# A perceiver layer on one core: three value tiles in every pair's turn, the keys between the probability transposes and the scores, and rows of scales in front of the scores

## The chip, the cores and the metric

The kernel runs on one core of one Trainium2 chip. The metric is the device time of one execution in microseconds (us), as the median of several runs of the same program.

## The reference, cut to what matters

The layer adds a cross attention, a causal self attention and a feed-forward part to a state of 2 batches x 128 rows x 512. The change touches the cross attention alone:

```python
xn = layer_norm(ctx, g1, b1)               # ctx: 2 x 2048 x 512
ln_lat = layer_norm(layernorm(x), g2, b2)  # 2 x 128 x 512
q = ln_lat @ Wq                            # 16 heads of 64
k, v = split(concat([xn, ln_lat]) @ Wkv)   # 2176 keys and values per batch
w = softmax(where(mask, (q * scale) @ (k * scale).T, -max))
x = x + (w @ v) @ Wout
```

## The kernel before, in words

**Precision.** Every projection is made with operands that are split into a high and a low part (`HI`, `LO`), by three products (`product`, L1629: high x high, high x low, low x high). So whatever TensorE projects into PSUM has to be split again before it is used: ScalarE copies the high part out of PSUM (a `*_hi` function), then VectorE subtracts it from PSUM to get the low part (a `*_lo` function). Only after the second of these is the PSUM bank free.

**Stages.** The 2176 columns of a batch are cut into three splits of 5 or 6 tiles of 128 columns, so there are 6 rounds (2 batches x 3 splits, `RNDS`). A round goes over 8 pairs of heads. `ITERS` = 48 turns follow each other, turn I being pair I % 8 of round I // 8; the text below calls rounds 0 and 3 the first splits, 1 and 4 the middle ones, 2 and 5 the last ones. Softmax is made online over the splits: a running maximum, a running sum, and an output that is scaled when the maximum moves. The first split of a batch needs no scaling, the middle one scales the output (alpha), the last one also divides by the sum (1/l).

**A turn on TensorE** (L1827 to L1862) works on three pairs at once. For pair I it transposes the probabilities (`turn_probs`, four calls into the four banks of pS and pT) and, after the scores, multiplies them with the values (`outputs`). For pair I + 1 it makes the scores (`scores`, into the same four banks). For pair I + 2 it makes the keys (`project_keys`, two chunks q = 0, 1 of up to 384 columns), and for the group of two pairs G = I // 2 + 1 a share of the values (`project_value`, one tile of 128 columns of context at a time, 12 matmuls each). In round 0 it also makes the queries of pair I + 2. `rows_of_scales` (L1774) turns alpha and 1/l into rows in bank pX; ScalarE copies them out (`scale_rows`), VectorE uses them in `merge`.

**Jobs.** Keys, values and queries all go through one PSUM tensor pJ with two banks. A list of jobs (L330) fixes their order and so the bank of each: job j uses bank j % 2 and TensorE waits in `job_bank` (L1674) until VectorE has taken the low part of job j - 2 (`c_jl`). Before, a group has three value jobs V.0, V.1, V.2 of two tiles each (the last of one tile where the split has five): V.0 in the even turn, V.1 and V.2 in the odd one.

**Keys are kept once.** KT holds one pair's keys for each q. So `key_hi` (L787) waits until `scores` of the pair before, same q, is done (`c_s`), and `scores` waits for `key_lo`.

**Order on the other engines.** ScalarE, turn I (L902): four `prob_hi`, `scale_rows`, `joined_hi`, `x_hi`, `value_hi`, `exps` of pair I + 1 (two, one per head, each needing the negated maxima of VectorE), `rescale` (alpha of pair I + 1), `value_hi` of V.2, `x_hi`, two `key_hi`. VectorE (L1314): `prob_lo`, `sums` (running sum and 1/l), three `prob_lo`, four `masked_max` of pair I + 1, `negate`, `value_lo`, `merge`, `value_lo` of V.2, `key_lo`, `join`, `stats` of a context chunk in every fourth turn, `key_lo`. GpSimd (L653) normalises a chunk (`normal`), takes low parts of the context (`x_lo`) and of the outputs (`joined_lo`). `steps_of` (L373) places the transposes of the next context chunk: in turns I = 0, 1, 4, 5, 8, 9 and so on up to 37, two `x_turn` each.

**Waits that count below.** `rows_of_scales` waits for alpha, and in the last splits for 1/l (`c_rec`, the end of `sums`). `outputs` waits for `merge` of the pair before. `join` waits for `joined_lo` of the pair before (`c_ol`). `x_turn` of a chunk waits for its `normal` (`c_norm`).

```python
def job_bank(name):
    j = job[name]
    if j >= 2:
        pe.wait_ge(c_jl, j - 1)
    return pJ[:, j % 2, :]
```

Of the kernel before, what the change touches and what calls it, by code (L numbers as in the profile page):

```python
# [35 lines left out]
def perceiver_layer(nc, x, ctx1024, mask, g1, b1, g2, b2, Wq, Wkv, Wout, qw, kw, vw, ow,  # L36
# [19 lines left out]
    PAIRS = H // 2  # L56
    SPLITS = 3
# [19 lines left out]
    with ExitStack() as stack:  # L77
# [251 lines left out]

        jobs = ["Q0", "K0.0", "V0.0", "K0.1", "V0.1", "V0.2", "Q1", "K1.0", "K1.1"]  # L330
        for I in range(ITERS):
            if I // 2 + 1 < GROUPS:
                jobs += [f"V{I // 2 + 1}.{I % 2}"]
            if I % 2 and I // 2 + 1 < GROUPS:
                jobs += [f"V{I // 2 + 1}.2"]
            if I + 2 < ITERS:
                jobs += [f"K{I + 2}.0", f"K{I + 2}.1"]
            if I + 2 < PAIRS:
                jobs += [f"Q{I + 2}"]
# [6 lines left out]
        def after_values(G):  # L346
            return job[f"V{G}.2"] + 1

        def after_round(R):
            return max(after_keys(PAIRS * R + PAIRS - 1), after_values(PAIRS // 2 * R + PAIRS // 2 - 1))  # L350

        def value_tiles(G, j):
            n = 5 if G // 4 % SPLITS == SPLITS - 1 else 6
            return list(range(2 * j, min(2 * j + 2, n)))

# [25 lines left out]
        def turned_before(I):  # L381

            return 4 + 2 * sum(steps_of(i) is not None for i in range(I))

        def scaled_before(C, k):

            if C < 2:
                return 0
            return sum(i // PAIRS % SPLITS > 0 for i in range(4 * C - (8 if k < 2 else 7) + 1))

# [343 lines left out]
        def _(act):  # L734
# [157 lines left out]
            value_hi(0, 1)  # L892
            value_hi(0, 2)
            exps(0, 0)
            exps(0, 1)
# [6 lines left out]
            for I in range(ITERS):  # L902
                n, step, G = I + 1, steps_of(I), I // 2 + 1
                for h in range(2):
                    for q in range(2):
                        prob_hi(I, h, q)
                scale_rows(I)
                if I >= 2 and pair_iter(I - 2):
                    joined_hi(I - 2)
                if step:  # L910
                    x_hi(step[0], step[1])
                if G < GROUPS:
                    value_hi(G, I % 2)
                if I + 3 < PAIRS:
                    wk_hi(I + 3)
                if n < ITERS:
                    exps(n, 0)
                    exps(n, 1)
                    rescale(n)
                if I % 2 and G < GROUPS:  # L920
                    value_hi(G, 2)
                if step:
                    x_hi(step[0], step[1] + 1)
                if I + 2 < ITERS:
                    key_hi(I + 2, 0)
                    key_hi(I + 2, 1)
                if I + 2 < PAIRS:
# [180 lines left out]
        def _(dve):  # L1108
# [199 lines left out]
            value_lo(0, 1)  # L1308
            value_lo(0, 2)
            query_lo(1)  # L1310
            key_lo(1, 0)
            key_lo(1, 1)

            for I in range(ITERS):  # L1314
                n, G = I + 1, I // 2 + 1
                C9 = (I + 10) // 4 if (I + 10) % 4 == 0 else 0
                prob_lo(I, 0, 0)
                sums(I)
                prob_lo(I, 0, 1)
                prob_lo(I, 1, 0)  # L1320
                prob_lo(I, 1, 1)
                if n < ITERS:
                    for q in range(2):
                        for h in range(2):
                            masked_max(n, q, h)
                    negate(n)
                if G < GROUPS:
                    value_lo(G, I % 2)
                if (I + 2) % PAIRS == 0 and (I + 2) // PAIRS < RNDS:
                    mask_bias((I + 2) // PAIRS)  # L1330
                merge(I)
                if I % 2 and G < GROUPS:
                    value_lo(G, 2)
                if I + 2 < ITERS:
                    key_lo(I + 2, 0)
                if I >= 1 and pair_iter(I - 1):
                    join(I - 1)
                if 3 <= C9 < CHUNKS:
                    stats(C9)
                if I + 2 < ITERS:  # L1340
                    key_lo(I + 2, 1)
                if I + 2 < PAIRS:
                    query_lo(I + 2)
# [282 lines left out]
        def _(pe):  # L1626
# [177 lines left out]
            scores(0, 1)  # L1804
            for i in (1, 2):
                for t in value_tiles(0, i):
                    project_value(0, i, t)
# [19 lines left out]
            for I in range(ITERS):  # L1827
                n, step, G = I + 1, steps_of(I), I // 2 + 1
                for h in range(2):
                    for q in range(2):  # L1830
                        turn_probs(I, h, q)
                rows_of_scales(I)
                if G < GROUPS:
                    ts = value_tiles(G, I % 2)
                    project_value(G, I % 2, ts[0])
                if step:
                    x_turn(step[0], step[1])
                if G < GROUPS:
                    project_value(G, I % 2, ts[1])
                if n < ITERS:  # L1840
# [7 lines left out]
                if step:  # L1848
                    x_turn(step[0], step[1] + 1)
                if I % 2 and G < GROUPS:  # L1850
                    for t in value_tiles(G, 2):
                        project_value(G, 2, t)
                if I + 2 < ITERS:
                    project_keys(I + 2, 0)
                    project_keys(I + 2, 1)
                elif I + 2 == ITERS:
                    pe.wait_ge(c_jl, NJ)
# [259 lines left out]
```

## Time and profile before

| | |
|---|---|
| runs of the program | 977.21 us median of 3 (975.59 to 979.12) |
| the profiled execution, its own time | 979.92 us |
| its span, first to last instruction | 978.1 us |
| TensorE matmuls busy | 874.0 us, 89% of the span |
| TensorE weight loads busy | 805.8 us, 82% |
| VectorE busy | 600.2 us, 61% |
| ScalarE busy | 491.4 us, 50% |
| GpSimd busy | 313.5 us, 32% |
| DMA | 99.11 MB, mean 101 GB/s |

The loop of 48 turns runs from 57.3 to 683 us of the span. The profiled execution took 2.7 us more than the median. In a row of a timeline the first number is the start in us of the span, the second the time in us; "[2.60 <-DVE xneg L1226]" is idle time of the engine before that row and who ended it. L numbers are lines of the kernel before. Most matmuls of the loop start 0.12 us (256 columns) or 0.17 us (384 columns) after each other and their records overlap, since each record also covers the way through the array.

### The profile page before, as it was taken

The page shows a single profiled execution, that of the slowest core. Times are in us where ns is not written, and L with a number is a line of the kernel's source. Part 1 is how long each engine was busy: PE and PEld are TensorE (multiplying, and loading weights), DVE is VectorE, ACT ScalarE, POOL GpSimd, SP SyncE. Part 2 cuts the span into 40 slices and gives each one's busy share as a digit, 9 for nine tenths or more (in the row PEclk, how much of TensorE's full clock was granted, in tenths as well). Part 3 has the DMA queues.
Part 4 walks back from the last instruction along what each step waited for, and adds up shares of the span by engine and source line. Part 5 has one row for each costly group of instructions (what it writes and reads, how often), then busy time and mean ns, then how long its engine had stood idle before and what let it go on. Part 6 is the DMA issues. An engine that isn't in the chain of part 4 may idle for free.

```text
span 978.1 us, 16973 instructions
## 1 busy us (share of the span) xinstructions
PE 874.0 (89%) x6217; PEld 805.8 (82%) x6217; DVE 600.2 (61%) x1550; ACT 491.4 (50%) x1051; POOL 313.5 (32%) x284
## 2 busy tenths in 40 slices
PE   3799999999998899999999999888687787978997
PEld 2699999999987888999999998887464586867885
DVE  6345546666657666555656666556286377865785
ACT  3465554645454554545454644454557154444553
POOL 3534522120202213131212000220726358753443
PEclk9799999999999999999999999999695888989999
DMA  5165321322323232322122223314220513421320
GB/s 191 58 222 184 123 98 65 109 90 87 108 90 128 72 122 91 120 91 99 69 82 90 87 87 133 123 40 145 100 87 0 188 47 126 130 86 64 109 87 22
DMA packets 45219, 99.11 MB, mean 101 GB/s; under 512 B 3745, under 2 KB 16977, under 8 KB 41937
## 3 DMA queue, kind: packets, MB, share of 16 engines
q1 hardware_dynamic: 45040, 98.00, 28.8%
q8 instruction: 50, 0.82, 0.3%
q14 instruction: 33, 0.26, 0.1%
q10 hardware_dynamic: 96, 0.02, 0.0%
HBM read 88.06 MB, written 8.91 MB: 99 GB/s over the span
## 4 chain that ended last, share of the span: by engine, by line
PE 75%; DVE 11%; issue 5%; ACT 4%; POOL 3%; DMA 1%; SPq 0%; DVEq 0%; ACTq 0%
PE pJ L1631 14%; PE pJ L1632 14%; PE pJ L1633 14%; PE pV L1770 7%; PE pS L1748 3%; PE pT L1756 3%; PE pS L1756 3%; PE pT L1748 2%; POOL WS L586 2%; PE pS L1631 2%; DVE KV L1119 2%; PE pS L1633 2%; PE pS L1632 2%; PE pX L1671 1%; PE pX L1787 1%
## 5 line engine op out<-in xcount | busy, mean ns | idle before, releaser
L1631 PE MATMUL pJ<-WV,XT 128*128 128x256 f32 x544 | 161.6, 297 | 0.0
L1632 PE MATMUL pJ<-WV,XT 128*128 128x256 f32 x544 | 154.9, 285 | 0.0
L1633 PE MATMUL pJ<-WV,XT 128*128 128x256 f32 x544 | 154.7, 284 | 0.0
L815 ACT ACTIVATE SP<-SP,xneg 128x768 f32<-128x768 f32 (+1 forms) x96 | 85.8, 895 | 115.7 <-DVE xneg L1226 115.7
L1631 PE MATMUL pJ<-XT,WK 128*128 128x384 f32 (+1 forms) x384 | 127.9, 333 | 5.0 <-POOL XT L609 2.6
L1633 PE MATMUL pJ<-XT,WK 128*128 128x384 f32 (+1 forms) x384 | 126.2, 329 | 0.0
L1632 PE MATMUL pJ<-XT,WK 128*128 128x384 f32 (+1 forms) x384 | 126.0, 328 | 0.0
L609 POOL TENSOR_TENSOR XT<-xtmp,XT 128x384 fp32r<-128x384 f32 (+1 forms) x44 | 41.3, 938 | 236.1 <-ACT XT L776 235.8
L1119 DVE TENSOR_TENSOR KT<-pJ,KT 128x384 fp32r<-128x384 f32 x96 | 51.0, 532 | 91.3 <-ACT KT L792 91.2
L1631 PEld LDWEIGHTS pJ<-WV,XT 128*128 128x128 f32 x544 | 105.4, 194 | 0.4 <-issue 0.4
L1632 PEld LDWEIGHTS pJ<-WV,XT 128*128 128x128 f32 x544 | 105.5, 194 | 0.0
L1633 PEld LDWEIGHTS pJ<-WV,XT 128*128 128x128 f32 x544 | 105.1, 193 | 0.0
L1220 DVE CUSTOM_DVE_ANT_0 SP<-pS,MB,mx 128x384 f32<-128x384 f32 x64 | 37.0, 616 | 77.5 <-PE pS L1748 77.5
L792 ACT ACTIVATE KT<-pJ 128x384 fp32r<-128x384 f32 x96 | 45.0, 470 | 72.1 <-PE pJ L1633 72.1
L799 ACT ACTIVATE VT<-pJ 128x512 fp32r<-128x512 f32 (+1 forms) x72 | 41.3, 574 | 74.3 <-PE pJ L1633 74.0
L1631 PEld LDWEIGHTS pJ<-XT,WK 128*128 128x128 f32 x384 | 73.1, 190 | 6.5 <-issue 2.9
L1770 PE MATMUL pV<-PT,VT 128*128 128x256 f32 x544 | 77.5, 291 | 0.0
L1770 PEld LDWEIGHTS pV<-PT,VT 128*128 128x128 f32 x544 | 67.7, 190 | 10.3 <-issue 7.9
L1632 PEld LDWEIGHTS pJ<-XT,WK 128*128 128x128 f32 x384 | 73.2, 191 | 0.0
L1633 PEld LDWEIGHTS pJ<-XT,WK 128*128 128x128 f32 x384 | 73.0, 190 | 0.0
L1119 DVE TENSOR_TENSOR VT<-pJ,VT 128x512 fp32r<-128x512 f32 (+1 forms) x72 | 47.2, 656 | 34.6 <-ACT VT L799 33.9
L1631 PE MATMUL pS<-XA,WS 128*128 128x256 f32 x176 | 52.9, 300 | 4.2 <-POOL WS L586 2.6
(344 smaller groups left out, 2196.3 us busy)
## 6 DMA issues: line engine op xcount, KB each, us to landing
WV<-wv_split SPq DMA_DIRECT2D x20, 1024.0 KB, 5.6
WK<-wk_split SPq DMA_DIRECT2D x40, 512.0 KB, 3.3
xraw<-in_ctx SPq DMA_DIRECT2D x7, 768.0 KB, 4.6
wk_split<-WK SPq DMA_DIRECT2D x8, 512.0 KB, 3.2
wv_split<-WV SPq DMA_DIRECT2D x4, 1024.0 KB, 6.2
wst<-in_L_ffn_Wg SPq DMA_DIRECT2D x4, 1024.0 KB, 5.1
raw<-in_L_ffn_Wu SPq DMA_DIRECT2D x4, 1024.0 KB, 5.8
work<-in_L_ffn_Wd SPq DMA_DIRECT2D x4, 1024.0 KB, 5.7
```

The costliest lines, as they stand in the source:

```text
L609: gp.tensor_tensor(XT[:, C % 4, LO, k, c0:c0 + w], xtmp[:, e % 2, 0:w], XT[:, C % 4, HI, k, c0:c0 + w].bitcast(F32), ALU.subtract).then_in ...
L792: ac.activation(KT[:, q, HI, 0:w], pJ[:, j % 2, 0:w], ACT.Copy).then_inc(c_jh, 1)
L799: ac.activation(VT[:, G % 2, ts[0]:ts[-1] + 1, :, HI, :], pJ[:, j % 2, 0:256 * len(ts)].rearrange("p (t h e) -> p t h e", t=len(ts), h=4), ...
L815: ac.activation(SP[:, I % 2, h, 0:w], SP[:, I % 2, h, 0:w], ACT.Exp, bias=xneg[:, I % 2, h:h + 1], scale=XSC, accum_out=total).then_inc(c_ ...
L1119: return ve.tensor_tensor(dst, src, hi.bitcast(F32), ALU.subtract)
L1220: ve.tensor_tensor_reduce(out=SP[:, n % 2, h, c0:c0 + w], in0=BANK[2 * q + h][:, 0:w], in1=MB[:, c0:c0 + w], scale=1.0, scalar=before, op0 ...
L1631: te.matmul(dst, a(HI), b(HI), start=start, stop=False)
L1632: te.matmul(dst, a(HI), b(LO), start=False, stop=False)
L1633: return te.matmul(dst, a(LO), b(HI), start=False, stop=stop)
L1748: last = te.matmul(BANK[2 * q + h][:, 0:w], Q[rows, qs, p, :], KT[rows, q, ks, 0:w], start=o == 0, stop=o == 2)
L1756: last = te.transpose(BANK[t % 4][:, P * i:P * i + P], SP[:, I % 2, h, CWID * q + P * i:CWID * q + P * i + P], ident[:, :])
L1770: last = te.matmul(pO[:, h, :, :], VT[:, G % 2, 3 * q + i, 2 * (I % 2) + h, :, :], PTS[t % 4][:, :, P * i:P * i + P], start=q == 0 and i = ...
```

## The change

TensorE's turn I becomes: transposes of the probabilities; the first `x_turn`; keys of pair I + 2; rows of scales; scores of pair I + 1; outputs of pair I; the second `x_turn`; three value tiles (two in the odd turns of a five-tile split); queries. The six value tiles of a group are now jobs of 2, 1, 2 and 1 tiles, two jobs in each turn. ScalarE and VectorE follow the new order of jobs: `key_hi` and `key_lo` of pair I + 2 stand in front of `exps` and `masked_max` of pair I + 1, `value_hi` and `value_lo` behind them. `sums` moves behind the fourth `prob_lo`, `stats` from the end of a turn to behind `sums` of the next one.

```diff
+        def value_tiles(G, j):
+            n = 5 if G // 4 % SPLITS == SPLITS - 1 else 6
+            return list(range((0, 2, 3, 5)[j], min((2, 3, 5, 6)[j], n)))
+        def value_jobs(G, js):
+            return [j for j in js if value_tiles(G, j)] if G < GROUPS else []
+        jobs = ["Q0", "K0.0", "V0.0", "K0.1", "V0.1", "V0.2", "V0.3", "Q1", "K1.0", "K1.1"]
         for I in range(ITERS):
-            if I // 2 + 1 < GROUPS:
-                jobs += [f"V{I // 2 + 1}.{I % 2}"]
-            if I % 2 and I // 2 + 1 < GROUPS:
-                jobs += [f"V{I // 2 + 1}.2"]
             if I + 2 < ITERS:
                 jobs += [f"K{I + 2}.0", f"K{I + 2}.1"]
+            jobs += [f"V{I // 2 + 1}.{j}" for j in value_jobs(I // 2 + 1, (2 * (I % 2), 2 * (I % 2) + 1))]
...
@@ ScalarE @@
                         prob_hi(I, h, q)
-                scale_rows(I)
+                if step:
+                    x_hi(step[0], step[1])
                 if I >= 2 and pair_iter(I - 2):
                     joined_hi(I - 2)
-                if step:
-                    x_hi(step[0], step[1])
-                if G < GROUPS:
-                    value_hi(G, I % 2)
+                if I + 2 < ITERS:
+                    key_hi(I + 2, 0)
+                    key_hi(I + 2, 1)
+                scale_rows(I)
                 if I + 3 < PAIRS:
                     wk_hi(I + 3)
                 if n < ITERS:
                     exps(n, 0)
                     exps(n, 1)
                     rescale(n)
-                if I % 2 and G < GROUPS:
-                    value_hi(G, 2)
                 if step:
                     x_hi(step[0], step[1] + 1)
-                if I + 2 < ITERS:
-                    key_hi(I + 2, 0)
-                    key_hi(I + 2, 1)
+                for j in value_jobs(G, (2 * (I % 2), 2 * (I % 2) + 1)):
+                    value_hi(G, j)
...
@@ VectorE @@
-                prob_lo(I, 0, 0)
+                for h in range(2):
+                    for q in range(2):
+                        prob_lo(I, h, q)
                 sums(I)
-                prob_lo(I, 0, 1)
-                prob_lo(I, 1, 0)
-                prob_lo(I, 1, 1)
+                if 3 <= C8 < CHUNKS:
+                    stats(C8)
+                if I + 2 < ITERS:
+                    key_lo(I + 2, 0)
+                    key_lo(I + 2, 1)
                 if n < ITERS:
                     for q in range(2):
                         for h in range(2):
                             masked_max(n, q, h)
                     negate(n)
-                if G < GROUPS:
-                    value_lo(G, I % 2)
...
                 merge(I)
-                if I % 2 and G < GROUPS:
-                    value_lo(G, 2)
-                if I + 2 < ITERS:
-                    key_lo(I + 2, 0)
                 if I >= 1 and pair_iter(I - 1):
                     join(I - 1)
-                if 3 <= C9 < CHUNKS:
-                    stats(C9)
-                if I + 2 < ITERS:
-                    key_lo(I + 2, 1)
+                for j in value_jobs(G, (2 * (I % 2), 2 * (I % 2) + 1)):
+                    value_lo(G, j)
...
@@ TensorE @@
                         turn_probs(I, h, q)
-                rows_of_scales(I)
-                if G < GROUPS:
-                    ts = value_tiles(G, I % 2)
-                    project_value(G, I % 2, ts[0])
                 if step:
                     x_turn(step[0], step[1])
-                if G < GROUPS:
-                    project_value(G, I % 2, ts[1])
+                if I + 2 < ITERS:
+                    project_keys(I + 2, 0)
+                    project_keys(I + 2, 1)
+                rows_of_scales(I)
                 if n < ITERS:
                     scores(n, 0)
                     scores(n, 1)
...
                 if step:
                     x_turn(step[0], step[1] + 1)
-                if I % 2 and G < GROUPS:
-                    for t in value_tiles(G, 2):
-                        project_value(G, 2, t)
-                if I + 2 < ITERS:
-                    project_keys(I + 2, 0)
-                    project_keys(I + 2, 1)
-                elif I + 2 == ITERS:
+                for j in value_jobs(G, (2 * (I % 2), 2 * (I % 2) + 1)):
+                    for t in value_tiles(G, j):
+                        project_value(G, j, t)
+                if I + 2 == ITERS:
```

The counts that other waits use (`after_values`, `turned_before`, `scaled_before`) follow the new order, and the stretch before the loop makes V0 in four jobs too.

## Rows read from the trace of the kernel before

**Rows 1.** The page: busy time by engine; one kind of DMA, KB each, us to landing.

```profile
PE 874.0 (89%) x6217; PEld 805.8 (82%) x6217; DVE 600.2 (61%) x1550; ACT 491.4 (50%) x1051; POOL 313.5 (32%) x284
...
WK<-wk_split SPq DMA_DIRECT2D x40, 512.0 KB, 3.3
```

**Rows 2.** Waits of TensorE from 40 to 690 us: total, times, longest (us).

```profile
PE pX L1787 <- issue: 24.8, 16, 3.1
...
PE pJ L1631 <- DVE KT L1119: 0.5, 2, 0.3
```

**Rows 3.** Stretches, one turn each (8, 10 and 19): us, busy by engine, clock, DMA.

```profile
170.86:182.95 12.09, 12.09 (x93) 11.67 (x92) 7.08 (x21) 7.95 (x18) 1.46 (x2) 1.00 0.35 131
197.92:209.35 11.43, 11.43 (x87) 11.02 (x86) 7.86 (x22) 5.60 (x14) 0.00 (x0) 1.00 0.36 139
...
310.49:325.99 15.50, 12.36 (x99) 11.54 (x97) 11.16 (x35) 6.02 (x16) 7.78 (x6) 1.00 0.15 45
```

**Rows 4.** Timeline of a middle split, turns 11 and 12, all engines.

```profile
213.84 0.79 PE L1748 MATMUL pS<-KT,Q 64*128 64x384 f32 x6
...
214.66 0.62 DVE L1220 CUSTOM_DVE_ANT_0 SP<-pS,MB,mx 128x384 f32<-128x384 f32 x1 [1.53 <-PE pS L1748]
...
216.62 0.28 PE L1631 MATMUL pJ<-WV,XT 128*128 128x256 f32 x1
...
217.14 0.94 ACT L815 ACTIVATE SP<-SP,xneg 128x768 f32<-128x768 f32 x1 [2.60 <-DVE xneg L1226]
...
219.00 0.46 ACT L828 ACTIVATE alpha<-mx,xneg 128x1 f32<-128x1 f32 x2
...
219.69 0.60 ACT L799 ACTIVATE VT<-pJ 128x512 fp32r<-128x512 f32 x1 [0.23 <-PE pJ L1633]
...
220.33 0.69 DVE L1119 TENSOR_TENSOR VT<-pJ,VT 128x512 fp32r<-128x512 f32 x1 [1.38 <-ACT VT L799]
...
221.78 0.49 ACT L792 ACTIVATE KT<-pJ 128x384 fp32r<-128x384 f32 x1 [1.48 <-PE pJ L1633]
...
222.30 0.56 DVE L1119 TENSOR_TENSOR KT<-pJ,KT 128x384 fp32r<-128x384 f32 x1 [1.29 <-ACT KT L792]
...
223.66 0.82 PE L1756 MATMUL pS<-ident,SP 128*128 128x128 f32 x6
...
224.97 0.38 PE L1787 MATMUL pX<-ident,alpha 128*128 128x128 f32 x2
```

**Rows 5.** Timeline of a first split, turn 25: VectorE, then ScalarE.

```profile
439.46 0.56 DVE L1220 CUSTOM_DVE_ANT_0 SP<-pS,MB 128x384 f32<-128x384 f32 x1 [2.29 <-PE pS L1748]
...
441.82 0.94 ACT L815 ACTIVATE SP<-SP,xneg 128x768 f32<-128x768 f32 x1 [2.48 <-DVE xneg L1226]
...
443.68 0.65 ACT L776 ACTIVATE xtmp<-pX,vec 128x384 f32<-128x384 f32 x1
...
444.79 0.48 ACT L792 ACTIVATE KT<-pJ 128x384 fp32r<-128x384 f32 x1
```

**Rows 6.** Timeline of a last split, turns 18 and 19.

```profile
304.58 0.80 PE L1748 MATMUL pS<-KT,Q 64*128 64x384 f32 x6
...
306.97 0.34 PE L1631 MATMUL pJ<-XT,WK 128*128 128x384 f32 x1
...
307.62 0.83 ACT L815 ACTIVATE SP<-SP,xneg 128x640 f32<-128x640 f32 x1 [2.33 <-DVE xneg L1226]
...
309.63 0.47 ACT L792 ACTIVATE KT<-pJ 128x384 fp32r<-128x384 f32 x1
...
311.22 1.88 DVE L1132 BATCH_NORM_STATS2 st<-xraw 128x6 f32<-128x512 f32 x3
...
314.84 6.20 POOL L622 TENSOR_SCALAR xraw<-xraw,mv,rstd 128x512 f32<-128x512 f32 x3
...
314.88 0.29 PE L1787 MATMUL pX<-ident,alpha 128*128 128x128 f32 x1 [3.14 <-issue]
```

**Rows 7.** A weight block split on ScalarE at the end of turn 44.

```profile
651.51 1.90 ACT L862 ACTIVATE XA<-raw 128x2048 fp32r<-128x2048 f32 x1
```

More of the change, by code:

```diff
@@ L346, in after_values @@
         def after_values(G):
-            return job[f"V{G}.2"] + 1
+            return job[f"V{G}.{value_jobs(G, range(4))[-1]}"] + 1
         def after_round(R):
             return max(after_keys(PAIRS * R + PAIRS - 1), after_values(PAIRS // 2 * R + PAIRS // 2 - 1))
-        def value_tiles(G, j):
-            n = 5 if G // 4 % SPLITS == SPLITS - 1 else 6
-            return list(range(2 * j, min(2 * j + 2, n)))
         def pair_index(I):
@@ L381, in turned_before @@
         def turned_before(I):
-            return 4 + 2 * sum(steps_of(i) is not None for i in range(I))
+            return 4 + 2 * sum(steps_of(i) is not None for i in range(I)) + (steps_of(I) is not None)
         def scaled_before(C, k):
@@ L388, in scaled_before @@
                 return 0
-            return sum(i // PAIRS % SPLITS > 0 for i in range(4 * C - (8 if k < 2 else 7) + 1))
+            return sum(i // PAIRS % SPLITS > 0 for i in range(4 * C - (8 if k < 2 else 7) + k % 2))
         @block.sync
@@ L893, in _ @@
             value_hi(0, 2)
+            value_hi(0, 3)
             exps(0, 0)
@@ L1309, in _ @@
             value_lo(0, 2)
+            value_lo(0, 3)
             query_lo(1)
@@ L1315, in _ @@
                 n, G = I + 1, I // 2 + 1
-                C9 = (I + 10) // 4 if (I + 10) % 4 == 0 else 0
-                prob_lo(I, 0, 0)
+                C8 = (I + 9) // 4 if (I + 9) % 4 == 0 else 0
+                for h in range(2):
+                    for q in range(2):
+                        prob_lo(I, h, q)
                 sums(I)
-                prob_lo(I, 0, 1)
-                prob_lo(I, 1, 0)
-                prob_lo(I, 1, 1)
+                if 3 <= C8 < CHUNKS:
[3 more added lines that the diff above has]
+                    key_lo(I + 2, 1)
                 if n < ITERS:
@@ L1804, in _ @@
             scores(0, 1)
-            for i in (1, 2):
+            for i in (1, 2, 3):
                 for t in value_tiles(0, i):
```

1 line of the change is left out of this document (removed).

## The prediction

> **What bounds the kernel now.** I read the page first: TensorE is busy 89% of the span and every other engine 61% or less [rows 1]. Then the waits of TensorE in the loop [rows 2]: one group stands out, 24.8 us in 16 waits, all in front of the rows of scales and all in the last splits, 8 in each batch. Next the stretches by turn [rows 3]: turn 10 is 11.43 us with TensorE busy for 11.43, so outside those waits the loop is a solid stream; turn 19 is 15.50 us with only 12.36 busy. Last the timelines. In turn 19 [rows 6] VectorE starts the statistics of the next context chunk at 311.22, in front of the low parts of the probabilities; `sums` comes behind them, and the rows of scales start at 314.88 after 3.14 us of idleness. TensorE's program order sets the end, so a change pays only through its waits.
>
> **The profiled execution** took 979.92 us, 2.7 us over the median of 977.21. I sum against it and shift at the end.
>
> **What the change removes.** The keys (24 matmuls, about 4 us) now stand between the transposes and the rows of scales. The longest old wait was 3.14 us [rows 2, 6], so 14 of the 16 waits go. The last two turns have no keys: of their two waits, 1.0 us each, nothing goes. 24.8 - 2.0 = 22.8 us. Two short waits of round 0 on a bank [rows 2] add 0.5: **23.3 us removed**. The matmuls are the same ones, in the same number. One more value job per six-tile group costs one copy and one subtraction on ScalarE and VectorE; both fall while TensorE makes keys, and should that cover be gone they cost at most their own 0.6 and 0.7 us [rows 4].
>
> **What the change adds.** I count from s, the start of the scores of pair I + 1, because KT holds one pair: the high part of the new keys may be copied only after those scores. Before, ScalarE and VectorE went from the scores straight to the maxima; now both halves of both key chunks stand in between.
>
> Middle splits [rows 4]. VectorE starts 0.82 us after s now (213.84 to 214.66). The first copy of keys can start at 0.9. The second needs the second chunk's scores, which are issued at 0.63 to 1.15 and end 0.4 later, 1.55. VectorE follows 0.52 behind ScalarE (221.78 to 222.30) and takes 0.53 for it: 2.60. So the maxima start 1.78 later than before. Exponentials began 3.30 after s (213.84 to 217.14): now 5.08. From there to the end of alpha 2.32 (217.14 to 219.00 + 0.46), and only then the copy of the first value job; VectorE 0.64 behind it, 0.69 long, 0.07 to TensorE. **The bank of the first value job is free at s + 8.80.** The next keys use that bank. TensorE is there at s + 2.78 for the first value (213.84 to 216.62), plus 36 matmuls of 0.12 = 4.32, plus transposes 1.31 (223.66 to 224.97): s + 8.41. It waits 0.39. The exponentials themselves are ready at about s + 6, before the transposes at 7.10, so they cost nothing in turns with three tiles.
>
> With an `x_turn` in the turn, ScalarE puts its two copies between alpha and the value copy: 1.11 us (443.68 to 444.79 [rows 5]). TensorE spends 0.33 per `x_turn` ((12.09 - 11.43) / 2 [rows 3]). In the first of two such turns the wait grows by 1.11 - 0.66 = 0.45, in the second by 1.11 - 0.33 = 0.78. Middle splits: 4 turns x 0.39 + 2 x 0.84 + 2 x 1.17 = 5.6, twice: **11.2 us**.
>
> First splits [rows 5]. No alpha, and maxima to exponentials take 2.36: bank free at 2.60 + 2.36 + 1.86 + 1.40 = 8.22, before 8.41. Turns without `x_turn` wait 0, the others 0.26 and 0.59; round 3 has two of each: **1.7 us**. In round 0 the queries stand right behind the values and use the bank of the first value job, which TensorE wants at s + 7.10: 1.12 in turns 2 and 3, 8.22 + 1.11 - 7.43 = 1.90 in turns 0, 1, 4 and 5: **9.8 us**.
>
> Last splits [rows 6]. The second chunk has two tiles: exponentials at 3.04 + 1.6 = 4.6, ready for the second head 1.85 later. The even turns have three tiles: bank free at about 8.1, wanted at 2.39 + 4.32 + 1.09 = 7.80: 0.3, with `x_turn` 0.75; 3.0 us for both rounds. The odd ones have two tiles and no second value job, so no bank wait, but the second head's transposes are wanted at 2.39 + 2.88 + 0.55 = 5.82 and its exponentials are ready at 6.45: 0.63, with `x_turn` 0.3; 4.4 us. **7.4 us**.
>
> Queues that the steps are moved past. `stats` moves to behind `sums` of the next turn, at about 3.4 us into it; from its start to the last `normal` are 9.8 us (311.22 to 314.84 + 6.20 [rows 6]), so a chunk is ready at 13.2. The first `x_turn` now stands right behind the transposes: after a full turn it is wanted at about 14, after short turn 19 at 12.2. There it waits 1.1. `joined_lo` sits behind `normal` on GpSimd, `join` waits for it, and the new order puts `value_lo` and the next `prob_lo` behind `join`: 0.3 more at turn 19, 0.5 at turn 23. **1.9 us**. At the end of turns 42 and 44 ScalarE splits a weight block, 1.90 us [rows 7], in front of the next `prob_hi`; with `sums` behind all four `prob_lo` 1/l is then 0.8 late: **1.6 us**. In turns 46 and 47 there are no keys as a cover, and `sums` moves behind three low parts, 1.2 us each: **2.4 us**. SyncE waits for `merge` in front of its next fetches, and `merge` moves later in the turn; keys are fetched two turns ahead, over 20 us, and land in 3.3 [rows 1]: nothing, and if that cover went, 3.3 each.
>
> Sum: 11.2 + 1.7 + 9.8 + 7.4 + 1.9 + 1.6 + 2.4 = 36.0 added, 23.3 removed: **+12.7 us**, 992.6 for the profiled execution, 990 for the median. The term that is not shown is the start of the copy of keys behind the scores. Its low bound is VectorE's 0.8 us for both chunks with none behind the other, which makes each of some 33 waits 0.4 shorter, -10 us in all; its high bound adds a hop of 0.2 on each engine, +8. I take the chained value since both engines run in order.
>
> **Rules of the skill.** The value job waits for a bank because pJ has only two. By the Trainium skill (Perfetto Trace Analysis, Identifying Performance Opportunities) the same gap repeating on the engine that should be full can mean that there is too little SBUF or PSUM for the next tile. Taken alone it would put a gap in every turn and the sum near the high end; the rows give none in 8 turns or so.
>
> TensorE's granted clock is 1.00 of 2.4 GHz in turn 19, though it idled for 3.14 us there [rows 3, 6]. The Trainium skill (TensorE: Matmul & The Clock Gate, Part 1) says that an idle TensorE falls back to half its clock. In turn 19 the trace shows no such fall, and the new waits are shorter.
>
> **Rivals.**
> - Covers hold (faster). ScalarE gets to the value copy early enough, by s + 7.0 in the middle splits and by s + 5.8 in round 0's turns without `x_turn`, and no bank wait arises. For it: ScalarE is busy for only half the span. Against it: 5.08 + 2.32 is already 7.4. Time: -23.3 + 2.4 (the last two turns) = 956, and between 956 and 974 if half of the waits stand.
> - About even: the waits are each 0.4 shorter, the sum -10 + 12.7 = +3: 977 to 980, since then the waits removed and added balance.
> - The clock falls. The new waits are many; if TensorE dropped to 1.2 GHz after each, a turn's 12 us would partly double. Against it: turn 19's clock. At 3 us more in a dozen turns, +36 on top: 1025.
> - The change doesn't do what it says: the rows of scales still wait since `sums` comes later by three low parts (1.2 us). They would have to be over 2.5 us late behind the keys; only turns 43 and 45 come near. The time would be about 1000.
>
> **Chances.** Forecast, with waits behind the value bank, 0.68, and slower; covers hold 0.20; even 0.09; clock or scales 0.03. About 0.3% (3 us) is what a measurement of this kernel can tell from no change. So faster 0.20, same 0.09, slower 0.71. The predicted time is that of the forecast, 990. The range takes in the bounds, 980 to 998, and reaches down through the even case to 973 and up to 1001.
>
> **What would show it.** In the changed profile: the waits in front of the rows of scales gone but for turns 43, 45, 46 and 47; new waits of TensorE in front of the first keys matmul and, in round 0, the queries, put down to VectorE's low part of values; turns of round 0 of about 15.1 us without `x_turn`; middle turns of 13.2; the exponentials 5.1 us behind the scores instead of 3.3; clock 1.00. It is wrong if TensorE's wait in front of keys and queries totals under 10 us, or if exponentials start less than 4.5 us behind the scores.

## The result and the profile after

| | before | after |
|---|---|---|
| median of four runs each | 976.81 us (975.59 to 979.12) | 982.88 us (981.52 to 984.20) |
| ratio | | 1.0059, 95% interval 1.0035 to 1.0084 |
| profiled execution, own time | 979.92 us | 984.20 us |
| its span | 978.1 us | 982.4 us |

The kernel is slower, by 6.1 us in the median and 4.3 us between the two profiled executions. The forecast was +12.7. The page of the kernel after, as [rows 1], and two of its costliest groups (idle time of the engine and its releaser stand last):

```profile
PE 880.2 (90%) x6217; PEld 805.0 (82%) x6217; DVE 597.2 (61%) x1566; ACT 482.3 (49%) x1067; POOL 314.0 (32%) x284
...
L1627 PE MATMUL pJ<-XT,WK 128*128 128x384 f32 (+1 forms) x384 | 130.4, 340 | 10.7 <-DVE VT L1118 6.0
...
L792 ACT ACTIVATE KT<-pJ 128x384 fp32r<-128x384 f32 x96 | 43.9, 473 | 171.8 <-PE pS L1744 166.1
```

The same number of matmuls, 16 more copies and 16 more subtractions. The last row names the new dependence: what ends the idle time in front of the copies of keys is now the scores (`pS`), where [rows 4] had the keys' own matmuls (`pJ`).

The waits of TensorE in the loop of the kernel after (40 to 695 us), against [rows 2]:

```profile
PE pJ L1627 <- DVE VT L1118: 15.2, 19, 1.9
PE pX L1783 <- issue: 6.1, 5, 3.0
PE pT L1744 <- DVE KT L1118: 1.2, 1, 1.2
PE pX L1667 <- POOLq L663: 1.1, 1, 1.1
PE pS L1752 <- ACT SP L815: 0.3, 1, 0.3
```

The 24.8 us in front of the rows of scales have become 6.1. In their place stand 15.2 us in 19 waits for the bank of the first value job. The third row lies ahead of the loop and is the same in the kernel before. Without it 22.7 us of waits stand against 25.3 [rows 2], and yet the kernel is slower. So this view alone doesn't give the answer, and I laid both kernels out by turn: a stretch goes from the first transpose of one turn to that of the next, read from each timeline, in us.

| turns | before | after | after less before | rows of scales alone (e1) |
|---|---|---|---|---|
| 0 to 5 (round 0) | 88.2 | 98.1 | +9.9 | 88.2 |
| 6, 7 | 25.3 | 25.4 | +0.1 | 25.3 |
| 8 to 15 (middle split) | 102.2 | 106.0 | +3.8 | 102.7 |
| 16 to 23 (last split) | 109.0 | 99.4 | -9.6 | 95.1 |
| 24 to 31 (first split) | 103.9 | 106.3 | +2.4 | 103.9 |
| 32 to 39 (middle split) | 102.2 | 105.9 | +3.7 | 102.7 |
| 40 to 45 (last split) | 78.9 | 69.4 | -9.5 | 67.1 |
| 46 | 8.0 | 13.1 | +5.1 | 8.0 |
| 47, to its outputs | 5.5 | 8.2 | +2.7 | 5.5 |
| start of outputs of turn 47, in the span | 680.7 | 689.6 | +8.9 | 655.9 |
| from there to the end | 297.4 | 292.8 | -4.6 | 295.0 |

**A middle turn.** Timeline of turn 10 of the kernel after, to be read against [rows 4]:

```profile
215.88 0.79 PE L1744 MATMUL pS<-KT,Q 64*128 64x384 f32 x6
...
216.80 1.01 ACT L792 ACTIVATE KT<-pJ 128x384 fp32r<-128x384 f32 x2 [4.50 <-PE pS L1744]
...
217.33 1.08 DVE L1118 TENSOR_TENSOR KT<-pJ,KT 128x384 fp32r<-128x384 f32 x2 [3.54 <-ACT KT L792]
...
218.32 0.61 DVE L1219 CUSTOM_DVE_ANT_0 SP<-pS,MB,mx 128x384 f32<-128x384 f32 x1
...
220.79 0.94 ACT L815 ACTIVATE SP<-SP,xneg 128x768 f32<-128x768 f32 x1 [2.70 <-DVE xneg L1225]
...
222.99 0.82 PE L1752 MATMUL pS<-ident,SP 128*128 128x128 f32 x6
223.02 0.84 ACT L799 ACTIVATE VT<-pJ 128x512 fp32r<-128x512 f32 x2
...
223.63 1.02 DVE L1118 TENSOR_TENSOR VT<-pJ,VT 128x512 fp32r<-128x512 f32 x2 [1.59 <-ACT VT L799]
...
224.37 0.45 PE L1627 MATMUL pJ<-XT,WK 128*128 128x384 f32 x1
```

From the start of the scores, s = 215.88: copy of keys +0.92, maxima +2.44, exponentials +4.91 (before: +3.30), value copy +7.14, its low part +7.75, next keys at +8.49. TensorE began its transposes at 222.99 and could have had the keys at 224.22: it is 0.15 late here. In the turns next to an `x_turn` the view has 0.4 to 0.7.

**The last two turns.** Timeline of turn 46 of the kernel after:

```profile
668.27 0.76 PE L1752 MATMUL pS<-ident,SP 128*128 128x128 f32 x5
...
669.31 0.57 ACT L799 ACTIVATE VT<-pJ 128x512 fp32r<-128x512 f32 x1
...
669.78 0.74 ACT L851 ACTIVATE PT<-pS 128x384 fp32r<-128x384 f32 x2
...
671.32 0.88 DVE L1118 TENSOR_TENSOR PT<-pT,PT 128x384 fp32r<-128x384 f32 x2
...
672.11 0.45 DVE L1237 TENSOR_SCALAR lsum<-lsum,alpha,rs 128x1 f32<-128x1 f32 x2
...
672.86 0.45 PE L1783 MATMUL pX<-ident,alpha 128*128 128x128 f32 x1 [3.01 <-issue]
...
673.88 1.33 PE L1744 MATMUL pS<-KT,Q 64*128 64x384 f32 x6
```

The copy of the last value job now stands in front of the copies of the probabilities, which begin 1.51 us behind the transposes, and `sums` comes behind all four low parts. With no keys as a cover TensorE waits 3.01 us. And the six score matmuls take 1.33 us where [rows 4] shows 0.79. The stretches of turns 46 (behind its wait) and 47 and the rest, with us, busy by engine, and the granted clock third from the end:

```profile
672.86:676.00 3.14, 3.14 (x17) 2.58 (x18) 0.76 (x3) 0.60 (x1) 0.00 (x0) 0.50 0.83 310
676.00:681.36 5.36, 5.36 (x22) 4.70 (x23) 3.56 (x13) 2.10 (x6) 0.00 (x0) 0.70 0.00 0
...
684.76:689.57 4.81, 4.81 (x17) 3.89 (x18) 0.00 (x0) 0.60 (x1) 0.00 (x0) 0.65 1.04 395
689.57:982.40 292.83, 236.54 (x1427) 196.97 (x1425) 191.70 (x409) 142.78 (x249) 152.31 (x130) 0.88 0.27 88
```

The clock fell to 0.50 of 2.4 GHz (the 1.2 GHz level) at the end of the wait. The kernel before held 1.00 through both turns. But it had a fall of its own in turn 45, behind a wait of 2.76 us, and this turn took 16.14 us where turn 43, with the same wait, took 14.89:

```profile
655.04 0.45 PE L1787 MATMUL pX<-ident,alpha 128*128 128x128 f32 x1 [2.76 <-issue]
...
651.03:667.17 16.14, 13.38 (x99) 12.72 (x98) 8.89 (x29) 7.76 (x17) 5.39 (x5) 0.89 0.02 5
...
667.17:680.70 13.53, 11.49 (x76) 9.61 (x75) 9.31 (x31) 6.88 (x19) 0.92 (x2) 1.00 0.46 154
680.70:978.10 297.40, 241.41 (x1427) 200.28 (x1425) 191.50 (x409) 143.02 (x249) 152.20 (x130) 0.86 0.27 91
```

**After the loop** the same 1427 matmuls take 236.5 us in the kernel after and 241.4 before, at mean clocks of 0.88 and 0.86. That difference of 4.9 is all of the 4.6 that the kernel after gains there. The change touches nothing in this part. Nor do e2 to e7 touch the stretch ahead of the loop, and it took 55.1 to 56.2 us in them and 57.8 in the kernel after: so two single executions can differ by 2 us in places that no edit reaches, and the parts of the loop are compared turn by turn.

### The profile page after: what moved, and what is told of

It is laid out like the page before. It is cut to its first block, busy times and chain, and to the rows that moved or that the text cites. A ratio compares the mean times of both kernels' runs of the same rounds, so it can differ in the third digit from the quotient of the medians.

```text
span 982.4 us, 17023 instructions
## 1 busy us (share of the span) xinstructions
PE 880.2 (90%) x6217; PEld 805.0 (82%) x6217; DVE 597.2 (61%) x1566; ACT 482.3 (49%) x1067; POOL 314.0 (32%) x284
## 4 chain that ended last, share of the span: by engine, by line
PE 56%; DVE 19%; issue 10%; ACT 9%; POOL 5%; DMA 1%; DVEq 0%; ACTq 0%; SPq 0%; POOLq 0%
PE pJ L1627 11%; PE pJ L1628 10%; PE pJ L1629 10%; PE pS L1744 3%; PE pV L1766 3%; DVE SP L1219 3%; PE pT L1752 2%; POOL WS L586 2%; DVE KV L1118 2%; PE pS L1627 2%; PE pS L1752 2%; ACT SP L815 2%; PE pS L1628 2%; DVE VT L1118 2%; PE pS L1629 2%
## 5 line engine op out<-in xcount | busy, mean ns | idle before, releaser
L1118 DVE TENSOR_TENSOR KT<-pJ,KT 128x384 fp32r<-128x384 f32 x96 | 48.9, 534 | 140.4 <-ACT KT L792 140.4
L1627 PE MATMUL pS<-XA,WS 128*128 128x256 f32 x176 | 52.9, 300 | 4.2 <-POOL WS L586 2.7
L622 POOL TENSOR_SCALAR xraw<-xraw,mv,rstd 128x512 f32<-128x512 f32 x27 | 56.2, 2092 | 0.9
L1628 PE MATMUL pS<-XA,WS 128*128 128x256 f32 x176 | 52.2, 297 | 0.0
```

The lines of the kernel that those rows point to most:

```text
L622: return gp.tensor_scalar(xraw[:, t, :], xraw[:, t, :], mv[:, t, 0:1], rstd[:, t:t + 1], ALU.subtract, ALU.mult)
L1118: return ve.tensor_tensor(dst, src, hi.bitcast(F32), ALU.subtract)
L1627: te.matmul(dst, a(HI), b(HI), start=start, stop=False)
L1628: te.matmul(dst, a(HI), b(LO), start=False, stop=False)
```

## The experiments

My theory after the result: one step of the change, the rows of scales, pays about 25 us, and the others give it back. They do so through the single KT: its copies wait for the scores, and maxima, exponentials and the value copies queue behind them. All times are medians of four runs or more; the kernel before had 978.67 us beside e1, e2, e4 and e5 and 977.52 beside e3, e6, e7 and e8. Ratios are to it, with the 95% interval. Beside the kernel after the kernel before had 976.81, so a difference of medians to the kernel after carries 1 to 2 us; by the ratios e5 is 20.6 us under it instead of 18.5, and e1 32.7 instead of 31.2. Diffs of e1 are to the kernel before, all others to the kernel after.

### e1: rows of scales in front of the scores, and nothing else

```diff
... (two counts for waits, turned_before and scaled_before, follow)
@@ ScalarE @@
-                scale_rows(I)
                 if I >= 2 and pair_iter(I - 2):
                     joined_hi(I - 2)
...
                     value_hi(G, I % 2)
+                scale_rows(I)
@@ TensorE @@
-                rows_of_scales(I)
                 if G < GROUPS:
                     ts = value_tiles(G, I % 2)
...
                     project_value(G, I % 2, ts[1])
+                rows_of_scales(I)
                 if n < ITERS:
                     scores(n, 0)
```

> The kernel before with one step of the change alone: rows_of_scales in front of the scores (behind the two value tiles), scale_rows behind value_hi. Theory A (the change removes the waits in front of the rows, and gives the gain back through its new order of keys, maxima, exponentials and value copies): most of the 24.8 us in front of the rows goes, since two value tiles (2.9 us) cover them; the start of turn 46 moves from 667.2 to about 646 and the time is near 956, 20 us under the kernel before. Rival B (the waits removed reappear anyway, at the scores or later, because VectorE's low parts are what the turn really waits for): the waits move to the scores, the time stays within 5 us of 977.

Measured: 951.70 us, ratio 0.9724 (0.9696 to 0.9752). The waits of TensorE:

```profile
PE pX L1787 <- issue: 2.3, 3, 1.0
```

24.8 us of waits became 2.3, the start of turn 46 came to 642.4 (646 expected), and the kernel beats both others. The two last splits shrank by 13.9 and 11.8 us, 25.7 in all, though the 14 waits that went add up to 22.8 in [rows 2]. Of the 2.9 us between, 1.25 are the fall of the clock in turn 45, which went too (16.14 to 12.03 us, where turn 43 went from 14.89 to 12.03). The other 13 waits, 20.0 us by their rows, gave back 21.6: up to 0.2 us more each (0.17 to 0.20 for the waits of 1.0 in turns 40, 41, 42 and 44, nothing for the two of 3.14 and 1.90 in turns 19 and 21). An idle time in such a row begins at the end of the last matmul's record, while the next one would have started before that end (a keys matmul's record is 0.34 long and the next starts after 0.17). So a wait can cost somewhat more than its row says.

### e2: queries in front of the values, in round 0

```diff
... (the list of jobs follows)
@@ TensorE; ScalarE and VectorE alike @@
                     x_turn(step[0], step[1] + 1)
+                if I + 2 < PAIRS:
+                    queries(I + 2)
                 for j in value_jobs(G, (2 * (I % 2), 2 * (I % 2) + 1)):
...
-                if I + 2 < PAIRS:
-                    queries(I + 2)
```

> The changed kernel with the queries of round 0 in front of the value tiles instead of behind them. Theory A (TensorE waits for the bank of the first value job): the 9.2 us of waits in front of the queries in turns 0 to 5 go, and turns 0 to 5 take 88 us together in place of 98.1 (a turn without x_turn 14.0 in place of 15.1); about 972 us. Rival B (round 0 is slow because ScalarE and GpSimd also split weights there, whatever the order of the banks): the waits move to the keys or the scores of the same turns, turns 0 to 5 stay over 95 us, and the time stays near 983.

Measured: 978.73 us, 1.0008 (0.9993 to 1.0023), a miss by 7 us, between the two expectations. Turns 0 to 5 took 95.8 us instead of 98.1, as the rival had it. Another 1.3 us of the gain on the kernel after lie in turn 46 (11.8 us instead of 13.1 with the same wait of 3.01), where the low clock lasted less long; the edit has no part in that. The first row is new:

```profile
PE pJ L1627 <- DVE Q L1118: 6.9, 6, 1.5
PE pX L1783 <- issue: 6.1, 5, 3.0
PE pJ L1627 <- DVE VT L1118: 5.9, 13, 0.7
```

The waits for the value bank fell by 9.3 us, but six waits of value tiles for the low part of the queries came: the second value job needs their bank, and they are copied behind the exponentials as well. In round 0 three jobs queue behind the exponentials for two banks, and another order only chooses which of them waits.

### e3: the second copy of context behind the value copies

```diff
@@ ScalarE @@
                     rescale(n)
-                if step:
-                    x_hi(step[0], step[1] + 1)
                 for j in value_jobs(G, (2 * (I % 2), 2 * (I % 2) + 1)):
                     value_hi(G, j)
+                if step:
+                    x_hi(step[0], step[1] + 1)
```

> The changed kernel with ScalarE's second x_hi behind the value copies instead of in front of them. Theory A: only the 20 turns with an x_turn gain, up to 1.1 us each less what TensorE's own x_turn had hidden: turns 0, 1, 4 and 5 about 0.9 each less, turns 8, 9, 12, 13 and their like 0.3 to 0.6 each; 8 us less in all, 975. The turns 2, 3, 6 and 7 don't move. Rival C: the copies of the next probabilities come 1.1 us later and the scores wait in their place, so the turns stay as they are and the time at 983.

Measured: 975.03 us, 0.9971 (0.9951 to 0.9991).

```profile
PE pJ L1627 <- DVE VT L1118: 5.2, 7, 1.8
...
PE pX L1667 <- ACT XT L776: 2.0, 6, 0.5
```

15.2 us of bank waits became 5.2, and the next `x_turn` now waits 2.0 for that late copy. Turns 0 to 5 fell from 98.1 to 95.1 us and turns 8 to 15 from 106.0 to 103.7. (Turn 3 took 17.2 us instead of 16.2, since behind its wait of 1.76 us the clock was 0.50 for 3.4 us; the kernel after has the same wait and no fall.) So `x_hi` in front of the value copy is a part of the bank waits, and a smaller one than the maxima are (e5): 7.9 us against 18.5.

### e4: sums behind the first low part again

```diff
@@ VectorE @@
-                for h in range(2):
-                    for q in range(2):
-                        prob_lo(I, h, q)
+                prob_lo(I, 0, 0)
                 sums(I)
+                prob_lo(I, 0, 1)
+                prob_lo(I, 1, 0)
+                prob_lo(I, 1, 1)
```

> The changed kernel with sums back behind the first of the four low parts of the probabilities. Theory A (sums behind four low parts makes 1/l about 1.2 us later, which shows only where no keys cover it): the wait in front of the rows falls from 3.0 to about 1.9 us in turn 46 and from 2.2 to 1.0 in turn 47, turns 43 and 45 lose their 0.3; 3 us less by the end of the loop, more if the clock then stays at 2.4 GHz, and 978 to 981 in all. Rival B (the tail is set by the copy of the last value job in front of the copies of the probabilities): under 1 us less.

Measured: 978.35 us, 1.0001 (0.9979 to 1.0023).

```profile
PE pX L1784 <- issue: 2.9, 2, 1.9
```

The time lies in the range of the first expectation, and so do the waits: of five (6.1 us) two are left, 1.9 us in turn 46 and 1.0 in turn 47. Behind the 1.9 us the clock still fell:

```profile
668.10:672.00 3.90, 3.89 (x20) 3.35 (x21) 2.53 (x10) 0.60 (x1) 0.18 (x1) 0.50 0.81 268
```

In turn 47 it was back at 1.00. The two last turns took 17.5 us, against 21.3 after and 13.5 before: that is most of the 4.5 us gained against the kernel after. The two last splits gave 0.9 each. Of the 1.9 us of turn 46 about 1.0 stood there before; the rest fits the value copy in front of the probability copies, which this kernel keeps.

### e5: half of the maxima in front of the first low part of keys

```diff
@@ VectorE @@
+                if n < ITERS:
+                    masked_max(n, 0, 0)
+                    masked_max(n, 0, 1)
                 if I + 2 < ITERS:
                     key_lo(I + 2, 0)
-                    key_lo(I + 2, 1)
                 if n < ITERS:
-                    for q in range(2):
-                        for h in range(2):
-                            masked_max(n, q, h)
+                    masked_max(n, 1, 0)
+                    masked_max(n, 1, 1)
                     negate(n)
+                if I + 2 < ITERS:
+                    key_lo(I + 2, 1)
```

> The changed kernel with VectorE's two maxima of a key chunk in front of the low part of the keys of the same chunk: max, max, key_lo 0, max, max, negate, key_lo 1. Theory A (the chain scores, copy and low part of the keys, maxima, exponentials, value copy, bank is what TensorE waits for): the exponentials start about 3.8 us behind the scores in place of 4.9, the bank of the first value job is free 1.1 us earlier, and nearly all waits in front of keys go; those in front of queries fall from 9.2 to about 4 us; 967 us, between 964 and 972. Rival B (the value copy is late for another reason: ScalarE's x_hi or its place behind key_hi): under 4 us less, 979 or more.

Measured: 964.36 us, 0.9848 (0.9818 to 0.9877).

```profile
PE pX L1786 <- issue: 5.4, 4, 2.5
...
PE pJ L1630 <- DVE VT L1118: 3.0, 5, 0.9
```

At the good edge of what was expected, and the largest single gain, 18.5 us against the kernel after, from an order on VectorE alone. The exponentials start 3.77 us behind the scores (3.8 expected). Turns 0 to 5 are back at 91.4 us, 8 to 15 at 102.6, which is what e1 has. About 1.0 us of the gain is a side effect: the negation of turn 3, held by GpSimd in the kernel after (last section), is not held here. So with the same work on TensorE, taking the two low parts of keys out of the way of the maxima is enough to end most bank waits. It is not the only way: e6 ends them further down the same chain.

### e6: the value copy between the two exponentials

```diff
@@ ScalarE @@
+                js = value_jobs(G, (2 * (I % 2), 2 * (I % 2) + 1))
                 if n < ITERS:
                     exps(n, 0)
+                if js:
+                    value_hi(G, js[0])
+                if n < ITERS:
                     exps(n, 1)
                     rescale(n)
...
-                for j in value_jobs(G, (2 * (I % 2), 2 * (I % 2) + 1)):
+                for j in js[1:]:
                     value_hi(G, j)
```

> The changed kernel with ScalarE's copy of the first value job between the two exponentials instead of behind alpha and x_hi. Nothing is taken from the maxima. Theory A (the bank of the first value job is freed late because its copy stands behind both exponentials, alpha and x_hi): the copy starts at about 5.9 us behind the scores in place of 7.1 to 8.3, the waits for the low part of values (15.2 us) go nearly all, round 0's turns 0 to 5 come near 88 to 90 us in place of 98.1; 966 us, 962 to 971. Rival C (it is VectorE that is late: the low part of the values stands behind merge and join): the waits shrink by less than a third, 978 or more.

Measured: 971.75 us, 0.9931 (0.9903 to 0.9959), just outside the expected range. Turns 0 to 5 took 89.6 us, as expected.

```profile
PE pT L1756 <- ACT SP L815: 6.4, 8, 0.9
PE pX L1787 <- issue: 5.6, 4, 2.3
PE pJ L1631 <- DVE VT L1122: 1.5, 2, 0.8
```

The bank waits are gone but for 1.5 us, as expected. Eight new waits came in front of transposes, for the second exponentials, all in the last splits, at the start of an even turn, behind a turn with two tiles: there is too little work on TensorE to cover a second exponential that comes 0.6 later. Turns 16 to 23 took 101.3 us instead of 99.4.

### e8: the old cut of the value jobs (2 tiles; 2 and 2), with the new order

```diff
         def value_tiles(G, j):
             n = 5 if G // 4 % SPLITS == SPLITS - 1 else 6
-            return list(range((0, 2, 3, 5)[j], min((2, 3, 5, 6)[j], n)))
+            return list(range(2 * j, min(2 * j + 2, n)))
         def value_jobs(G, js):
-            return [j for j in js if value_tiles(G, j)] if G < GROUPS else []
+            return {(0, 1): [0], (2, 3): [1, 2]}.get(tuple(js), [0, 1, 2]) if G < GROUPS else []
... (the stretch before the loop makes V0 in three jobs)
```

> The changed kernel with the values cut as before: one job of two tiles in the even turns, two jobs in the odd turns, all behind the outputs; keys and rows of scales stay where the change puts them. Theory A (what costs is the second value job of every turn, which makes the next keys or queries wait for the first one's bank): in the even turns the next keys and queries use a bank that keys had, so those waits go; in the odd turns two more tiles cover them. In exchange the exponentials are late for the transposes in even turns without queries, 0.6 us each. Turns 0 to 5 near 89 us in place of 98.1, waits of 0.5 to 0.8 in front of transposes in about 17 turns; 969 us, 964 to 974. Rival D (the three tiles are what keeps the long chain of maxima and exponentials covered, as the change has it): the two-tile turns wait over 1.5 us each, and the time is at 990 or over.

Measured: 977.47 us, 1.0002 (0.9983 to 1.0021). Neither expectation holds in full.

```profile
PE pX L1781 <- issue: 6.7, 4, 2.4
...
PE pX L1665 <- ACT XT L776: 3.8, 8, 0.7
PE pJ L1625 <- DVE VT L1117: 3.3, 6, 1.3
```

Round 0 went as expected, 89.1 us: with one value job in the even turns the queries find their bank free. The middle splits stayed at 105.9. The even turns are now a tile shorter, and what ends late there is no bank but `x_hi` for the next `x_turn`. And the last splits grew (turns 16 to 23 from 99.4 to 103.2 us), which cancels most of round 0's gain; in turn 20 the clock also fell, behind waits of 0.9 and 1.3. So three tiles a turn are worth something under this order, and outside round 0 the cut alone is not the cause.

### e7: e3, e4 and e5 together

> The changed kernel with three edits together: maxima in front of the low part of the keys, sums behind the first low part of the probabilities, second x_hi behind the value copies. Theory A: the waits are of one chain, so what each edit gives does not add up; after the first edit (964) there are left about 3 us in round 0, 2 us in the last two turns, 0.7 in turns 43 and 45 and 1.5 at turn 20: about 958, and not under the 951.7 of the kernel before with the rows moved alone. Rival: they add up fully (-18, -4, -8) and give 953 or less.

Measured: 958.63 us, 0.9807 (0.9769 to 0.9845), as expected.

```profile
PE pX L1787 <- issue: 2.4, 2, 1.4
PE pX L1671 <- ACT XT L776: 1.9, 6, 0.5
```

Turn 46 now waits 1.39 us for the rows, and the clock holds:

```profile
648.38:656.80 8.42, 7.03 (x50) 5.85 (x49) 7.54 (x26) 4.94 (x14) 0.45 (x1) 1.00 0.43 132
```

Turn 46 takes 8.4 us, as before (8.0). Of the 31.2 us between e1 and the kernel after, these three edits win back 24.3. What is left, 6.9 us, is the price of the rest of the change: keys in front of the scores, the second value job, the new place of `stats`. No run separates these. By turns it lies mostly in 16 to 23 (97.8 us against 95.1 in e1) and 24 to 31 (105.9 against 103.9). A second KT should take away the wait of the copies for the scores. It was not tried.

## Why the prediction was right and wrong

**The direction and the main mechanism were right, the size was not.** The kernel is slower, 982.9 us lies in the range, and the new waits are those named: for VectorE's low part of values, in front of keys and, in round 0, of queries. Of the signs, turn 2 took 15.14 us (15.1 forecast), the middle turns 13.25 in the mean (13.2, but this mean also holds turns with an `x_turn` and two short ones, so it confirms little), the exponentials came 4.91 behind the scores (5.1), the rows of scales wait in turns 43, 45, 46 and 47 and, not forecast, 0.42 us in turn 18. The rival "covers hold" fell: it asked for the value copy at s + 7.0, and that came at 7.14 without `x_turn` and later with it. It was near. "Clock 1.00" did not hold in the last two turns.

**The size was half of the forecast.** In the terms of the sum, up to the outputs of turn 47 (us):

| term | forecast | measured | from |
|---|---|---|---|
| removed by rows of scales | -23.3 | -24.8 | e1 less before, 655.9 - 680.7; 1.25 of it is the clock in turn 45 |
| added, turns 0 to 45 | +33.6 | +25.9 | after less e1 at turn 46, 668.3 - 642.4; 0.4 of it ahead of turn 0 |
| added, turns 46 and 47 | +2.4 | +7.8 | table by turn |
| loop | +12.7 | +8.9 | |
| after the loop | 0 | -4.6 | same matmuls, another clock |
| profiled execution | +12.7 | +4.3 | |

- *Added in turns 0 to 45.* The step that failed is the length of the chain from the scores to the value bank and to the second exponentials, in the middle and last splits. The middle splits added 3.3 and 3.2 against e1 instead of 5.6 each. The last ones added 4.3 and 2.3 instead of 5.9 and 5.0. The chain was summed from whole records, with the bank free for TensorE at s + 8.80. The keys that waited for it started at s + 8.49, and without a wait they would have started at 8.34 (8.41 forecast). Of the 0.31 us, 0.07 are a wait of the second copy of keys for its own scores, which the forecast put at 1.55 and which end at 1.32, so that this copy starts at 1.45 right behind the first. The rest is records added end to end, while the pieces follow each other a little before the record in front ends (maxima at 2.44, the low part of keys in front ending at 2.53; 2.23 from exponentials to value copy, where records gave 2.32; value copy to low part 0.61 instead of 0.64). The sum with the low bound, 10 us less, was near in number, but not by its reason: that bound took 0.4 off the start of the maxima, and the chip 0.16.
- *Round 0 and round 3* came out as forecast (9.9 for 9.8, 2.4 for 1.7), partly by luck. The chain was too long there as well: turns 0, 1, 4 and 5 added 6.8 instead of 7.6. Turn 3 made up for it with 1.0 us that nobody had forecast, a held negation (last section). In round 3, 0.9 us lie in turn 24, whose keys wait 0.64 for turn 23's low part of values; the forecast had 0.5 for this, among the last splits.
- *The second exponentials* of the odd turns in the last splits, 0.63 us each in the forecast, show up as one wait of 0.3 in the view of waits. Their two operations of 640 columns take 1.64 us together (turns 40 to 45); the forecast used 1.85, near the 1.86 of the 768-column ones, and had them start at 4.6 where they started at 4.45. In e6, with 0.6 us more in front of them, they do show, at up to 0.9: the margin was real and small.
- *The last two turns* cost 7.8 us instead of 2.4, and most of the difference is a term that the sum put at nothing, the clock. Their waits grew by 2.0 and 1.1 (1.02 to 3.01 and 1.02 to 2.15), the turns by 5.1 and 2.7: the other 4.7 us are matmuls at the low clock. The waits were under-counted by less, 3.1 for 2.4. Moving `sums` behind three low parts cost the 1.1 or 1.2 that were priced (e4 gives 1.13 back in each turn). Not priced was ScalarE's queue in turn 46: the copy of the last value job stands in front of the copies of the probabilities. By e4 this is about 0.9 us of the 3.01, argued and not tested alone.
- *The clock.* I took turn 19, idle for 3.14 us at 1.00, as showing that waits up to this length are safe. Turn 46 was idle for 3.01 us and went to 0.50. The trace of the kernel before already had the counter-example, turn 45 at 0.50 behind 2.76 us, while turns 23 and 43 held 1.00 behind the same 2.76. By the Trainium skill (TensorE: Matmul & The Clock Gate, Part 1) an idle TensorE falls back to half its clock. Turn 46 agrees and turn 19 does not, so one undisturbed gap is no proof for the next. With waits of 1.9 in e4 the clock fell, with 1.4 in e7 it did not, and with 1.76 in turn 3 it fell in e3 and held in the kernel after. So length alone does not decide. Why 3.14 us were safe in turn 19 is open.
- *After the loop* nothing was forecast. The profiled executions of all ten kernels take between 292.4 and 297.4 us there with the same program; the kernel before happens to have the longest and the kernel after nearly the shortest. By the medians the difference of the kernels is 6.1 us, between the 8.9 of the loop and the 4.3 of the whole. So of the 6.6 us between forecast and medians the terms of the loop explain 3.8, in which errors of -8 and +5 partly cancel, and what made up the rest in the other executions stays open.

**The rule on bubbles** (the Trainium skill, Perfetto Trace Analysis, Identifying Performance Opportunities) fits what happened: the repeated gap in front of the keys was one of two PSUM banks not yet free. But the runs show that more banks are not the only cure (a third was not tried). e5 took 12.2 of the 15.2 us of these waits away with the same two, by freeing them earlier.

## What to carry to other kernels

Split a change into its parts before believing its name: here the part that cured the wait shown by the profile was worth 27 us alone (e1 against before), and the rest of the same change cost 31 (after against e1). When a copy out of PSUM writes to an operand kept once, write down what it waits for and all that its engine's queue has behind it: maxima, exponentials and the next bank's copy moved 1.6 us with it, and one swap on VectorE returned 18 us. Go through the last iterations of a pipelined loop one by one, since a queue that is covered by a next iteration's work is bare there. And a wait can also cost the clock: 2.0 us more of waiting in turn 46 brought 3.1 us more of slow matmuls.

## What the runs showed of the hardware that I had not expected

**A tiny VectorE operation can be held for as long as a GpSimd one lasts.** In turn 3 the queries waited 1.76 us where turn 2 waited 0.74. The timeline of the kernel after:

```profile
116.27 1.30 POOL L593 TENSOR_TENSOR WK<-wkst,WK 128x512 fp32r<-128x512 f32 x1
...
116.39 1.20 DVE L1225 TENSOR_SCALAR xneg<-mx 128x2 f32<-128x2 f32 x1
```

The negation of 2 columns takes 0.17 us where nothing holds it. Here it took 1.20 and ended at 117.59, when GpSimd's subtraction ended at 117.57. The exponentials waited for it. By the Trainium skill (SBUF — State Buffer, SBUF: two separate sides) the two engines share a pair of SBUF ports that one holds for a whole instruction while the other is blocked; this row agrees, with 1.03 us lost by an operation of 0.17. e2, e3, e4, e6 and e8 have the same row in turn 3, at 1.13 to 1.20; e5 and e7, where the negation starts earlier, have not. In other turns of all kernels negations are held as well. Under GpSimd's normalisation of 2.08 us they do not wait for its end, so here the measurement is not what the page says. The kernel before:

```profile
107.11 2.09 POOL L622 TENSOR_SCALAR xraw<-xraw,mv,rstd 128x512 f32<-128x512 f32 x1
107.25 0.64 DVE L1226 TENSOR_SCALAR xneg<-mx 128x2 f32<-128x2 f32 x1
```

It ended 0.78 us behind the start of the normalisation, and so, within 0.01, did every negation in the ten traces that started 0.15 to 0.56 behind one. Those that started 0.78 to 1.37 behind it took 0.17, and those at 1.54 to 1.87 ended with it. No experiment was made for this, and GpSimd's records are rough.

**A wait can cost up to 0.2 us more than its idle row,** as e1 showed: 21.6 us back for 20.0 us of rows in 13 waits, the turn with the fall of the clock left out.
